# Five shared PSUM banks, taken in turn by the engine that empties them

## The reference, cut to what matters

```
h  = layernorm(x) * (1 + ca) + sa            # per sequence
xn = layernorm(h) * ln1_w + ln1_b
# attention: 16 heads of 8 channels, causal, softmax
scores = einsum('bqhd,bkhd->bhqk', q, k) * 8 ** -0.5
attn_out = (softmax(scores masked) @ v) @ o_w + o_b
# state space branch: 256 channels, 16 states
x_c = silu(causal_conv4(x_ssm) + conv_b);  dt = softplus(x_dbc[:8] @ dt_w + dt_b)
h_t = exp(dt_t * A) * h_{t-1} + (x_t * dt_t) * B_t ;  y_t = C_t . h_t
ssm_out = ((y + x_c * D) * silu(z)) @ ssm_out_w
h = h + alpha * attn_out + (1 - alpha) * ssm_out
```

## Time and profile before

| | |
|---|---|
| median of 3 runs | 1898.97 us |
| profiled execution | 1907.24 us, its span 1905.5 us |
| PE, DVE, ACT, POOL busy | 78%, 72%, 56%, 45% of the span |
| norms beside the first branches | about 55 to 85 us |
| attention and state space together | about 104 to 1063 us |
| attention alone, the end of the stage | 1063 to 1105 us |
| feed-forward, experts, layer 1 (not touched) | from 1105 us |

### The profile page before, as it was taken

One profiled execution on the slowest core, in us unless ns is written; L12 is line 12 of the kernel. 1 busy time (PEld: TensorE's weight loads), 2 busy tenths in 40 slices (PEclk: granted clock), 3 DMA queues, 4 the chain that ended last, 5 costly groups with the idle time before them and its releaser, 6 DMA issues. The chain is left out here.

```text
span 1905.5 us, 21890 instructions
## 1 busy us (share of the span) xinstructions
PE 1479.4 (78%) x7090; PEld 913.6 (48%) x7090; DVE 1380.0 (72%) x2071; ACT 1073.2 (56%) x1784; POOL 854.0 (45%) x866
## 2 busy tenths in 40 slices
PE   4856767767677677677676778879999999988778
PEld 3323433333334343343343346447878787744573
DVE  2587877868868688687789348587767777748866
ACT  3734555555465455554655456468787878842107
POOL 3273646647455466464666321121222222227753
PEclk9866888989888798798889989889999999976889
DMA  3121112111121021111210020101111111100001
GB/s 79 54 80 51 58 34 65 56 50 58 47 65 62 20 65 56 54 58 42 70 56 23 1 74 26 53 13 46 45 39 50 39 45 45 45 6 1 1 1 44
DMA packets 61654, 84.72 MB, mean 44 GB/s; under 512 B 6588, under 2 KB 32038, under 8 KB 61542
## 3 DMA queue, kind: packets, MB, share of 16 engines
q1 hardware_dynamic: 61442, 83.30, 13.9%
q10 hardware_dynamic: 100, 0.03, 0.0%
HBM read 74.38 MB, written 8.78 MB: 44 GB/s over the span
## 5 line engine op out<-in xcount | busy, mean ns | idle before, releaser
L994 PE MATMUL bank<-QK 127*128 127x128 bf16 (+7 forms) x1024 | 255.5, 332 | 173.5 <-DVE Mx L1243 119.1
L1554 ACT ACTIVATE bank<-dtv,alog 128x512 f32<-128x512 f32 x256 | 176.3, 690 | 285.4 <-DVE hst L1263 284.6
L1686 POOL TENSOR_TENSOR dBx<-dtx,Bb 128x512 f32<-128x512 f32 x256 | 321.9, 1279 | 16.0 <-DMA Bb<-b_dram 9.4
L1296 DVE TENSOR_TENSOR hl<-lsq,hh 128x512 fp32r<-128x512 f32 x320 | 251.2, 794 | 90.7 <-ACT hh L1570 83.0
L1263 DVE TENSOR_TENSOR_SCAN hst<-bank,dBx 128x512 f32<-128x512 f32 x256 | 297.8, 1204 | 4.3 <-POOL dBx L1686 4.3
L1567 ACT ACTIVATE lsq<-bank,vcol 128x512 f32<-128x512 f32 x320 | 219.4, 692 | 111.8 <-DVE hl L1296 62.0
L1243 DVE TENSOR_REDUCE Mx<-bank 128x1 f32<-128x384 f32 (+3 forms) x352 | 216.9, 628 | 78.9 <-PE bank L994 77.7
L1666 POOL TENSOR_SCALAR_AFFINE_SELECT PT<-PT 128x256 f32<-128x256 f32 (+1 forms) x320 | 118.5, 376 | 345.8 <-ACT PT L1510 344.0
L994 PEld LDWEIGHTS bank<-QK 127*128 127x128 bf16 (+1 forms) x1024 | 93.8, 107 | 334.8 <-DVE Mx L1243 178.1
L1181 DVE SCALAR_TENSOR_TENSOR yT<-bank,bc,yT 128x256 f32<-128x256 f32 x480 | 200.5, 475 | 59.2 <-PE bank L1097 58.5
L1705 POOL TENSOR_TENSOR stage<-stage,lrs 128x512 f32<-128x512 f32 x64 | 93.7, 1464 | 309.2 <-DVE lrs L1376 309.2
(11 more groups left out here) (248 smaller groups left out, 2467.3 us busy)
## 6 DMA issues: line engine op xcount, KB each, us to landing
Bb<-b_dram SPq DMA_DIRECT2D x128, 256.0 KB, 3.4
stage<-w_rows SPq DMA_DIRECT2D x64, 256.0 KB, 3.2
parts<-part SPq DMA_DIRECT2D x16, 384.0 KB, 2.8
QK<-parts SPq DMA_DIRECT2D x64, 96.0 KB
QK<-parts SPq DMA_DIRECT2D x64, 64.0 KB
stage<-in_L_ffn_We_dram SPq DMA_DIRECT2D x16, 256.0 KB, 3.2
hst<-in_L_attn_x_dram SPq DMA_DIRECT2D x8, 256.0 KB, 5.6
QK<-parts SPq DMA_DIRECT2D x64, 32.0 KB
```

The source lines that it names most:

```text
L994: return engine.matmul(o, l, r, start=start, stop=stop, tile_position=pos, skip_group_check=True)
L1296: engine.tensor_tensor(hl[:, sl, :], full[:, f, :], hh[:, sl, :].bitcast(F32), ALU.subtract).then_inc(sems["dve_hl"], 1)
L1554: engine.activation(bank[4 + h][:], dtv[:, b % 2, h, :], ACT.Exp, scale=alog[:, h, n:n + 1]).then_inc(sems["act_da"], 1)
L1686: engine.tensor_tensor(dBx[:, sl, h], dtx[:, b % 2, h], Bb[:, sl], ALU.mult).then_inc(sems["pool_dbx"], 1)
```

## The change

The two rings by branch become two rings by the engine that empties the bank: banks 0 and 1 (`to_act`) for all that ScalarE empties, banks 2, 6 and 7 (`to_dve`) for all that VectorE empties. The norms' centring banks, which VectorE frees, become 2, 3, 2, 3 in place of 0, 1, 2, 3. Nothing is computed otherwise and the order of the steps is the same.

```diff
-    ring, ring2 = [0, 1, 2], [0]
+    ring_act, ring_dve = [0, 1], [2, 6, 7]
-    def take():
-        ring.append(ring.pop(0))
-        return ring[-1]
-    def take2():
-        ring2[0] += 1
-        return 6 + (ring2[0] - 1) % 2
+    def to_act():
+        ring_act.append(ring_act.pop(0))
+        return ring_act[-1]
+    def to_dve():
+        ring_dve.append(ring_dve.pop(0))
+        return ring_dve[-1]
...
# qk0, val, maxrow, on, att        : take()  -> to_act()
# max, wo                          : take()  -> to_dve()
# bx, bz, dt, first bank of dbc    : take2() -> to_act()
# second bank of dbc, yt, so       : take2() -> to_dve()
...
-            k = take2()
+            k = to_dve() if n else to_act()
             it = step("acc", g=g, half=half, bank=k, ...
...
-    banks = ((0, 4), (1, 5), (2, 4), (3, 5))
+    banks = ((2, 4), (3, 5), (2, 4), (3, 5))
```

More of the change, by code:

```diff
@@ L138, in plan_mixers @@
     late, later, pts = [], [], [0]
-    def take():
-        ring.append(ring.pop(0))
-        return ring[-1]
-    def take2():
-        ring2[0] += 1
-        return 6 + (ring2[0] - 1) % 2
+    def to_act():
[4 more added lines that the diff above has]
+        return ring_dve[-1]
     def project(b):
         for i in range(2):
-            k = take()
+            k = to_act()
             it = step("qk0", b=b, i=i, bank=k, free=free.get(f"b{k}"), ready=r_n[b], qf=free.get("qf"), part=free.get("part"))
@@ L182, in maxima @@
             for q in range(2):
-                k = take()
+                k = to_dve()
                 it = step("max", u=u, q=q, qi=qi, a=a, heads=n, bank=k, free=free.get(f"b{k}"), ready=r_qk[u], mx_free=free.get(f"Mx{s2}"))
@@ L290, in steps_of @@
         pb = b % 2
-        k, k2 = take2(), take2()
+        k, k2 = to_act(), to_dve()
         it = step("dbc", b=b, bank=k, bank2=k2, free=free.get(f"b{k}"), free2=free.get(f"b{k2}"), xc=("act_silu", 2 * b + 1),
```

## The result

The changed kernel took 1913.53 us (median of 20 runs, 1892.62 to 1921.58), the kernel before 1900.06 us (20 runs, 1892.73 to 1906.46). The ratio after to before is 1.0056, 95% interval 1.0034 to 1.0079: some 10.6 us slower, where 8 were forecast. It is taken over all runs in the fast state (18 and 20) and is not the quotient of the medians, which is 1.007, or 13.5 us. The profiled execution of the changed kernel took 1912.56 us, its span is 1910.8.

What follows compares the result with a forecast made beforehand. No engine bounds it throughout: ScalarE bounds the norms, VectorE's busy plus idle time sets the blocks. Norms +33, blocks -28 and attention's end +3 gave +8 us, 1907 us on the median; range 1868 to 1932.

Steps and rivals of the forecast that it cites:

- The norms: Norms beside the first branches: two centring banks make them one chain, a third of intervals at low clock; +33 us.
- The block: Repeating block of one sequence in the mixer stage: gains and losses from the regrouped rings sum to -4.0 us per block.
- bz: Step in the block: no longer waits for yT, so TensorE's 4.17 us stall goes; -2.9 us per block.
- The bx copies and hT: In the block, acc no longer waits for copies of bx, and a later hT wait goes; -1.6 us for both.
- dt: Step in the block: no longer waits for yT, and ScalarE starts its chain earlier; -1.4 us per block.
- scan, max, max, acc: In the block: acc no longer comes late behind an att waiting for the first maximum; -1.0 us per block.
- on: Attention's denominators' matmul: waits in ScalarE's ring behind copies held by the decay, 0.75 later twice; +1.6 us per block.
- acc of state 0: In the block: goes to ScalarE's ring, so an already late maximum comes 0.5 us later.
- att behind bz: In the block: att waits for the copy of bz in ScalarE's ring; +0.6 us.
- The two that should stay: VectorE gaps in the block: 4.88 us (an exp behind silu) and 4.81 us (matmuls of dbc), expected unchanged.
- The end of the attention: Attention running alone: with two banks each ScalarE exp waits 0.1 us more, about 30 times; +3 us (0 to 8).
- Rival 2: In the blocks, VectorE finds work after every scan, two thirds of 97 us waits go; 1863 us, chance 0.25.

Runs made afterwards that it cites:

- branch_in_old_ring: Kernel before with steps bx, bz and dt taking banks from the old ring of three instead of banks 6 and 7; ratio to before 0.9927.
- on_in_bank3: Changed kernel with the norms' centring banks 2, 3, 6, 7 and the attention's denominators' matmul in just-emptied bank 3; ratio to before 0.9625.

## Why the prediction was right

**The norms: right in mechanism, +28.85 for +33.** The chain is there, 4.21 us per norm at the full clock where the sum of its parts gave 4.11 (from the centring to the mean matmul it is 0.96, 81.44 to 82.40, and not 0.86). Eleven intervals were chained and not twelve: the last product follows the one before by 1.25 us, for no further norm starts between them. Four of the eleven were longer, 4.92 to 6.01 us, so a third at the low clock was somewhat high: they are longer by 4.9 us in all, where the forecast had 7.5. In four other profiled executions with two banks the last product starts at 115.73 to 117.02, so +31.3 to +32.5, the forecast's size. The Trainium skill (Perfetto Trace Analysis, "Matmul Optimizations") says that the engine scales its power with its use, and the prediction took from it that the pauses would hold the chain at the low clock. The trace agrees in part, since behind pauses of the same 2.23 us it shows both 2.07 us (75.43) and 1.12 us (85.65) for the two matmul records of a centring.

**The block: -2.9 us per interval for -4.0.** The repeat is 123.0 us for 126.25, or -3.2, 2.5 of it in VectorE's idle time and 0.8 in its busy time, which I did not follow up. The seven intervals gained 20.55 us, not 7 x 3.2, for not all of the kernel before took 126.25: I read one block and multiplied it, and two of its neighbours had 123. By the terms, idle before and after:

- bz: -2.9 forecast, -3.1 in the profile (the 3.09 is gone). The bx copies and hT: -1.6 and -1.6 (0.69 and 0.93 gone). dt: -1.4 forecast, -1.8 found, the 0.87 and two small gaps of 0.34 and 0.60 (at 679.71 and 681.97). bz and dt were the sound part: their gaps are there in the short block of the kernel before too, and branch_in_old_ring took the 0.87 away and half of the 3.09. The 0.69 is missing in that short block, so it is not shown to be the work of the rings.
- scan, max, max, acc: -1.0 forecast, about 0 found. The 0.96 went, but the maximum and the conv after it came 0.40 and 0.59 late. (In the short block of the kernel before the 0.96 is 0.33.)
- "on": +1.6 forecast, +3.6 found, the term that was mis-sized most. The maxima after it are late by 3.45 and 2.19 for 1.50 and 1.27, and the yT behind the first by 0.72 more. I priced the later release, and the low clock only for the second of the two, where it was before; the first now stands for 3.26 us and then takes 2.05 us, against 1.10 in the kernel before. on_in_bank3 shows the whole price of that step in the new rings, 5.1 us per interval against the long blocks and 2.6 against the short ones.
- acc of state 0: +0.5 forecast; 0.92 and 1.94 became one gap of 3.21, +0.35. att behind bz: +0.6 forecast; +0.9 at its yT, -0.65 at the next maximum. wo: +0.45 and +0.27.
- The two that should stay did: 5.27 for 4.88 and 4.52 for 4.81.

**The end of the attention: +2.6 for +3** (186.3 for 183.7), and in the second execution +0.5. All of the +2.6 lies in the attention that runs alone: from the eighth copy into bc to the last product into xc, where the scans end, both kernels took 142.0 us.

Together +28.85 - 20.55 + 2.6 = +10.9 us at the end of the stage (the spans differ by 5.3 only, since the stages behind it, which the change doesn't touch, took 5.6 less in that execution); the ratios say +10.6 us in one comparison and +2.5 in the other (1.0013), where the interval takes in 1. That the number came so close is in part luck. The norms lost 4 us less than forecast and the blocks gained 7 less, and the two errors partly cancel. And the sum knew nothing of the two lengths of block: 3.5 us seven times over, the step from 123.0 to 119.4, is 25 us, three times the forecast difference. Rival 2 needed over 5 us per block. It was right in one thing: the waits were there to be had, 758.4 us for 828.2. But 20.5 of these 70 us came with the new rings, and the other 49 with taking "on" and state 0 out of ScalarE's ring.

## What to carry to other kernels

- A ring of banks should be judged by what each step in it waits for at its turn. The step to take out first is the one that stands in the ring at a bad turn and has a bank of its own at hand: one line, "on" in the bank it had just emptied, was worth 2.9% in the old rings, more than the whole regrouping (1.8% with four banks for the norms).
- Banks taken from a phase that pipelines more deeply (norm n+2 starts before n+1 ends, so two banks made it one chain) can cost more than the loop gains; count the steps in flight in every phase that shares the pool.
- Before multiplying one period, look at several: here the same kernel repeats at 119.4 us in one execution and at 123 in another.

## What the runs showed that was not expected

- The block's length and the clock go together, in one and the same kernel. The same wait of 3.26 us left the matmuls behind it at 2.05 us in one execution and 1.28 in another, and the block kept to 123.0 or 119.4 us over the last four repeats. Among 20 runs of the changed kernel the span goes with the mean granted clock: 1916.5 and 1918.4 us at 0.868, 1900.9 and 1903.2 at 0.890, 1890.9 at 0.901. Which of the two is the cause these runs don't separate.
- The chained norms, with 2.2 us pauses between their matmuls, were granted 2.4 GHz in most of the intervals: seven of eleven took 4.21 us.
